# A two-layer graph network: the first layer's one-hot tiles move from VectorE to GpSimd, between its gathers

## The reference

```
h = relu(layernorm(x))
ef = (relu(edge_attr @ We1 + be1) @ We2 + be2) * sigmoid(edge_weight * Wt + bt)
msg = relu(concat(h[src], ef) @ Wn1 + bn1) @ Wn2 + bn2
x = x + h + segment_sum(msg, dst)                  # first layer
g = relu(layernorm(x))
y = g + segment_sum(g[src], dst)
x = x + relu(relu(y @ W1 + b1) @ W2 + b2)          # second layer
```

## Time and profile before

| | |
|---|---|
| median of 3 runs | 2865.11 us |
| the profiled execution: its span, from first to last instruction (no other time of it is recorded) | 3603.9 us |
| mean granted TensorE clock in it | 0.804 of full speed |
| busy share of the span: PE, PEld, DVE, ACT, POOL | 74%, 45%, 54%, 28%, 58% |
| GpSimd: gathers | 2080, 2032.9 us busy, 977 ns mean |
| DMA | 426.82 MB, mean 118 GB/s |

### The profile page before, as it was taken

The page is one execution under the profiler, slowest core; times in us unless marked ns, Lnnn a source line. Parts: engine busy times, 40 slices in busy tenths (PEclk is TensorE's granted clock), DMA queues, the critical chain, the costliest instruction groups (busy, mean ns, idle before and its releaser), DMA issues.

```text
span 3603.9 us, 51709 instructions
## 1 busy us (share of the span) xinstructions
PE 2652.8 (74%) x14584; PEld 1610.3 (45%) x14585; DVE 1962.6 (54%) x4063; ACT 1009.1 (28%) x1000; POOL 2098.5 (58%) x2125
## 2 busy tenths in 40 slices
PE   4687788877877778778877788785645766766766
PEld 3344444444444444444444444343332545544544
DVE  8665566655656566656655566665673333233333
ACT  3233333333333333333333333232231111111112
POOL 6566666666666666666666665555254555555552
PEclk8788888888888888878888888887875777877777
DMA  6444444444433343444344343333122434334332
GB/s 196 113 127 134 127 127 136 125 130 128 126 121 125 123 124 122 123 125 124 120 122 128 120 128 115 120 117 96 32 101 83 132 118 129 122 95 128 101 114 61
DMA packets 229418, 426.82 MB, mean 118 GB/s; under 512 B 82703, under 2 KB 141584, under 8 KB 229072
## 3 DMA queue, kind: packets, MB, share of 16 engines
q0 software_dynamic: 74752, 153.23, 16.3%
q1 hardware_dynamic: 103152, 177.42, 15.0%
q10 hardware_dynamic: 51266, 93.34, 7.4%
HBM read 364.35 MB, written 59.43 MB: 118 GB/s over the span
## 4 chain that ended last, share of the span: by engine, by line
PE 39%; issue 20%; DVE 17%; another core or an unknown queue 12%; DVEq 10%; SPq 1%; DMA 1%; ACT 0%; POOL 0%; ACTq 0%
PE ps L925 9%; PE ps L836 8%; PE ps L795 8%; DVE nodes L1185 5%; PE ps L804 5%; PE ps L815 4%; PE ps L787 3%; DVEq L1119 3%; DVEq L1165 2%; DVE hot L1140 2%; DVE acc L1127 1%; DVE arena L1185 1%; DVEq L1182 1%; PE ps L915 1%
## 5 line engine op out<-in xcount | busy, mean ns | idle before, releaser
L537 POOL DMA_INDIRECT big<-table,idx x2080 | 2032.9, 977 | 1375.8 <-issue 587.6
L836 PE MATMUL ps<-nodes 128*128 128x500 bf16 x1280 | 448.5, 469 | 335.8 <-DVE nodes L1185 180.3
L795 PE MATMUL ps<-arena,we 128*128 128x512 f32 x784 | 511.9, 784 | 29.7 <-issue 12.2
L640 ACT ACTIVATE big<-big 128x1024 f32<-128x1024 f32 x196 | 207.2, 1057 | 1074.3 <-DVE big L1134 917.5
L815 PE MATMUL ps<-hot,big 128*128 128x64 f32 x3136 | 395.9, 275 | 112.8 <-issue 86.0
L1185 DVE TENSOR_SCALAR nodes<-iota_k,win_off,nodes 128x500 bf16<-128x500 f16 x1280 | 453.7, 407 | 0.0
L815 PEld LDWEIGHTS ps<-hot,big 128*128 128x128 f32 x3136 | 381.6, 195 | 107.0 <-issue 104.6
L1182 DVE TENSOR_TENSOR nodes<-iota_b,nodes 128x384 bf16<-128x384 f16 (+1 forms) x492 | 245.4, 499 | 266.8 <-remote 174.8
L1134 DVE TENSOR_TENSOR big<-ps,big 128x1024 f32<-128x1024 f32 x196 | 239.3, 1221 | 244.2 <-issue 242.6
L836 PEld LDWEIGHTS ps<-nodes 128*128 128x128 bf16 x1280 | 106.3, 106 | 573.6 <-DVE nodes L1185 271.1
L630 ACT ACTIVATE arena<-ps,cols 128x1024 f32<-128x1024 f32 x196 | 218.5, 1115 | 418.7 <-PE ps L787 229.2
(11 more groups left out here) (147 smaller groups left out, 2534.2 us busy)
## 6 DMA issues: line engine op xcount, KB each, us to landing
arena<-in_ew SPq DMA_DIRECT2D x196, 512.0 KB
arena<-in_ea SPq DMA_DIRECT2D x196, 256.0 KB
counts_d<-arena ACTq DMA_DIRECT2D x192, 245.0 KB
acc<-counts_d ACTq DMA_DIRECT2D x15, 2940.0 KB
big<-table,idx POOLq DMA_INDIRECT x2080
table<-big SPq DMA_DIRECT2D x7, 672.0 KB, 3.0
idx<-in_src SPq DMA_DIRECT2D x260, 4.0 KB
xs<-in_x SPq DMA_DIRECT2D x7, 448.0 KB, 5.5
```

The lines of the kernel that those rows point to most:

```text
L537: pool.indirect_dma_start(to(u, q, t), None, table, bass.IndirectOffsetOnAxis(ap=idx[:, u, at:at + 1], axis=0))\
L795: pe.matmul(p_ef[q], we2[:, :], hid[:, q, :], start=True, stop=True).then_inc(ef_mm, 1)
L836: m = pe.matmul(to, hots[:, t, :], keys[:, t, :], start=False, stop=True, skip_group_check=True)
```

## The change

GpSimd makes the first layer's one-hots, a tile at a time (`tile_hots`, 128x64, 8 a pair, 1568 in all), and VectorE's `pair_hots0` is gone from this pass (it stays in later sweeps over the edges, which only run for graphs with wide blocks). From the fourth pair on, a one-hot follows each gather: with the gathers of pair p go the one-hots of pair p-3. The last three pairs' one-hots follow the last gather. GpSimd no longer waits for `ef_mm`, and its one wait for `agg_mm` ahead of pair p is for the sums of pair p-5, which used the same half of `hot`. `hot_made` counts tiles instead of blocks, and VectorE tells by `windows_moved` that `rel` is made. TensorE increments `hid_mm`, `ef_mm` and `pre_mm` once a pair by 2, where it did twice by 1. The second layer is as it was.

```diff
+            HOTS_BACK = RING - 1
+            for pair in range(NPAIR):
+                u, b = pair % RING, pair // RING
+                if b:
+                    pool.wait_ge(pre_made, 2 * (pair - RING) + 2)
+                pool.wait_ge(idx_loaded[u], b * 16 + 16)
+                if b:
+                    pool.wait_ge(agg_mm, pair - HOTS_BACK - 1)
+                    pool.sem_inc(pairs_begun, 1)
+                if pair == HOTS_BACK:
+                    pool.wait_ge(windows_moved, 1)
+                for q in (0, 1):
+                    for t in range(TB):
+                        gather_one(table0, to_rows, u, q, t, gathered)
+                        if pair >= HOTS_BACK:
+                            tile_hots(pair - HOTS_BACK, q, t)
+            for pair in range(NPAIR - HOTS_BACK, NPAIR):
+                pool.wait_ge(agg_mm, pair - 1)
+                for q in (0, 1):
+                    for t in range(TB):
+                        tile_hots(pair, q, t)
...
-                    if not free:
-                        pool.wait_ge(ef_mm, b * (2 * RING) + 2 * u)
                     pool.sem_inc(pairs_begun, 1)
-                    gather_block(table0, to_rows, u, 0, gathered)
-                    if not free:
-                        pool.wait_ge(agg_mm, b * RING + (u - 2))
-                    pool.sem_inc(pairs_begun, 1)
-                    gather_block(table0, to_rows, u, 1, gathered)
...
+            def tile_hots(pair, q, t):
+                at = pair * (2 * TB) + q * TB + t
+                pool.tensor_scalar(hot[:, pair % 2, q, t, :], iota_s[:, :], rel[:, at:at + 1], None, ALU.is_equal)\
+                    .then_inc(hot_made, 1)
...
-                    pe.matmul(p_ef[q], we2[:, :], hid[:, q, :], start=True, stop=True).then_inc(ef_mm, 1)
+                    i = pe.matmul(p_ef[q], we2[:, :], hid[:, q, :], start=True, stop=True)
+                i.then_inc(ef_mm, 2)
...
                 if since >= 2:
-                    pair_hots0(b if u >= 2 else b - 1, (u - 2) % RING)
+                    if not first:
+                        pair_hots0(b if u >= 2 else b - 1, (u - 2) % RING)
                     sum_hots(n - 4, u % 2)
```

More of the change, by code:

```diff
@@ L532, in _, with gather_one @@
                 pool.tensor_tensor(x_g, x_g, stages[g % 2], ALU.add).then_inc(xh_made, 1)
+            def gather_one(table, to, u, q, t, landed):
+                at = q * TB + t
+                pool.indirect_dma_start(
+                    to(u, q, t), None, table,
+                    bass.IndirectOffsetOnAxis(ap=idx[:, u, at:at + 1], axis=0))\
+                    .then_inc(landed[u][q], 16)
             def gather_block(table, to, u, q, landed):
                 for t in range(TB):
[L536 to L540, removed]
+                    gather_one(table, to, u, q, t, landed)
             def gather_pair(table, to, u, landed):
@@ L552, in _, with gather_body @@
             pool.wait_ge(table0_stored, 16 * NG)
[L553 to L557, removed]
+            def tile_hots(pair, q, t):
[23 more added lines that the diff above has]
+                        tile_hots(pair, q, t)
+            def gather_body(b):
                 for u in range(RING):
@@ L560, in gather_body @@
                     pool.wait_ge(idx_loaded[u], b * 16 + 16)
-                    if not free:
-                        pool.wait_ge(ef_mm, b * (2 * RING) + 2 * u)
                     pool.sem_inc(pairs_begun, 1)
-                    gather_block(table0, to_rows, u, 0, gathered)
-                    if not free:
-                        pool.wait_ge(agg_mm, b * RING + (u - 2))
-                    pool.sem_inc(pairs_begun, 1)
-                    gather_block(table0, to_rows, u, 1, gathered)
-            for b in range(1, NBODY):
-                gather_body(b, b >= NBODY - 2)
+                    gather_pair(table0, to_rows, u, gathered)
             pool.wait_ge(sweeps_made, 1)
@@ L786, in hidden_products @@
                     k = slice(q * K_EDGE, (q + 1) * K_EDGE)
-                    pe.matmul(p_hid[q], we1[k, :], ea_s[k, u, :], start=True, stop=True).then_inc(hid_mm, 1)
+                    i = pe.matmul(p_hid[q], we1[k, :], ea_s[k, u, :], start=True, stop=True)
+                i.then_inc(hid_mm, 2)
             def edge_products(n, first):
@@ L805, in message_products @@
                                       start=True, stop=True)
-                    i.then_inc(pre_mm, 1)
+                i.then_inc(pre_mm, 2)
             def aggregate(n, m, first):
                 pe.wait_ge(msg_made, n + 2)
-                pe.wait_ge(hot_made, n + 2)
+                pe.wait_ge(hot_made, n * TB + 2 * TB)
                 if not first:
@@ L1113, in _ @@
             first_windows()
+            dve.sem_inc(windows_moved, 1)
             dve.wait_ge(acc_zeroed, 1)
@@ L1140, in pair_hots0 @@
                 dve.tensor_tensor(hot[:, u % 2, :, :, :].rearrange("p q t w -> p (q t) w"), iota_t, r, ALU.is_equal)\
-                   .then_inc(hot_made, 2)
+                   .then_inc(hot_made, 2 * TB)
             def sum_hots(n, m):
-                dve.wait_ge(hot_made, n + 2)
+                dve.wait_ge(hot_made, n * TB + 2 * TB)
                 with nc.allow_low_precision("sums of four zeros and ones"):
@@ L1211, in edge_keys, with pair_step @@
                 settle()
-            def pair_step(s, b, u, since, counted=False):
+            def pair_step(s, b, u, since, first, windows=False):
                 blk = b * (2 * RING) + 2 * u
                 n = s * NB + blk
-                if counted:
+                if windows:
                     window_hots(window_entry(early_group(b, u), VTS[u]), hot_src0, hot_key0, src_b0, key0, VTS[u], VH)
@@ L1257, in sweep @@
                 for u in range(RING):
-                    pair_step(s, 0, u, u)
+                    pair_step(s, 0, u, u, counted)
                     if counted and u < NWG:
@@ L1266, in sweep @@
                         for u in range(RING):
-                            pair_step(s, b, u, RING, True)
+                            pair_step(s, b, u, RING, True, True)
                 else:
@@ L1270, in sweep @@
                         for u in range(RING):
-                            pair_step(s, b, u, RING)
+                            pair_step(s, b, u, RING, False)
                 messages(s * NB + (NB - 4), s, NBODY - 1, RING - 2)
                 add_sums(s * NB + (NB - 6), NB - 6, s * NPAIR + (NPAIR - 2))
-                pair_hots0(NBODY - 1, RING - 2)
+                if not counted:
+                    pair_hots0(NBODY - 1, RING - 2)
                 sum_hots(s * NB + (NB - 4), 0)
@@ L1277, in sweep @@
                 add_sums(s * NB + (NB - 4), NB - 4, s * NPAIR + (NPAIR - 1))
-                pair_hots0(NBODY - 1, RING - 1)
+                if not counted:
+                    pair_hots0(NBODY - 1, RING - 1)
                 sum_hots(s * NB + (NB - 2), 1)
```

## The result

| | us, median | range | runs |
|---|---|---|---|
| kernel before, measured beside the changed one | 2866.45 | 2864.87 to 2877.59 | 4 |
| changed kernel | 3632.01 | 3630.59 to 3636.18 | 4 |
| ratio | 1.268 | 1.265 to 1.270 | |

Slower by 766 us. Predicted were 3200 us, 2860 to 3420. The sign is right, the size is 2.3 times too small, and the time lies outside the range.

The account below looks back on a forecast made before the run. GpSimd's back-to-back gathers were taken to bound both layers of the timed run, some 85% sure. 2865 us plus 329 for the one-hots plus 6 at the layer's end gave 3200, range 2860 to 3420.

Parts of the forecast that it names:

- the sum: Whole kernel before: GpSimd's gathers back to back, plus gaps and ends, 2867.7 us; the second layer's part 644.7.
- Rival C: Whole kernel: GpSimd doesn't bound the timed run, so the kernel gains, 2732 us at best; chance 0.10.
- The one-hot's own cost: First layer, GpSimd: each 128x64 one-hot takes 0.21 us, 329 us for 1568; between 204 and 392 by kind.
- Meetings with VectorE: First layer: one-hots wait for VectorE's use of SBUF, 0.05 us each, 78 us, kept for the range only.
- VectorE's 133.5 us: First layer: one-hots taken off VectorE, 133.5 us less work there, worth nothing while GpSimd bounds.
- the removed waits: First layer: GpSimd's dropped waits for other engines, worth 0 in a timed run, at most 71 us.
- the new waits: First layer: VectorE's sum of pair p-3 waits for pair p's gathers; chain 6.7 to 9.9 us, doesn't decide.
- the increments: TensorE: three fewer increments a pair, worth nothing, since TensorE has 2 us a pair to spare.
- The end of the layer: End of first layer: 24 one-hots after the last gather, 5 us, and a chain of waits; 6 us more.
- B: Between gathers: the one-hot fits in the 0.30 us gap, gathers stay at 1.25; 2871 us, or 2800 to 2875; chance 0.15.
- D: Between gathers: a one-hot prevents the overlap of the next gather's start, 0.81 us each, 4140 us; chance 0.10 with milder form.
- its milder form: First layer: SBUF ports met at each one-hot, 0.41 us each on 2871, 3514 us; shares the 0.10 chance.

Follow-up runs that it names:

- experiment 5: Kernel before with one or four of a pair's eight first-layer gathers left out (0.946, 0.818), or one-column instructions added behind every fourth, second, or every gather (0.994, 0.990, 0.977).
- experiment 2: Changed kernel with the instruction between gathers replaced: 64-column write 3728.46 us, copy 3736.64, one-column comparison 3593.96, comparison with a constant 3764.28.
- experiment 3: Changed kernel with a pair's eight one-hots behind its eight gathers instead of one behind each: 3763.39 us, ratio 1.044 to the kernel before.

## Why the prediction came out as it did

*What bounds.* Borne out for the timed run, which is the first chip's, though no trace shows that run. The changed kernel's second layer is the same code, measured beside it, and took 649.3 us for the 644.7 of the sum, and what the other stages leave for the first layer of before is 1.30 us a gather, near the 1.25 of gathers back to back. Rival C (2732 us) is out. The profile that I read was of the other pace, in which GpSimd's work doesn't bound (experiment 5); the change costs 7% there, and 1.784 us a gather is only 0.17 more than the 1.61 of that profile.

*The one-hot's own cost.* This is the step that failed: "I take 0.21, nearer to the row that reads: 1568 x 0.21 = 329 us", with ends of kind of 0.13 and 0.25. It is 0.45, 706 us, more than twice the 0.21. Neither row was of its kind. IOTA writes only, and experiment 2 shows that a write-only instruction nearly vanishes in a gather's turn. The select's 0.25 us for 128 columns was no ceiling either: a comparison costs 0.285 with a single column, and 2.6 ns more with each further one. The Trainium skill (GPSIMD Engine Reference, section 3.1 "Elementwise — side-by-side cycle accounting") states about 1.8 cycles an element at best and 2.6 with two inputs, at 1.2 GHz; by these figures an element is 1.5 to 2.2 ns, an estimate. The 2.6 ns measured here are 3.1 such cycles, somewhat above.

*Meetings with VectorE.* I kept 78 us for the range and added none. The mean distance of 1.784 is 0.084 above the regular 1.70, 132 us in 1568. The trace of the changed kernel shows where they lie: some 95 us in 435 distances that are less than 1 us too long, and some 38 in nine longer holes, one of 22.9 near the layer's end. Of the 238 distances that are 0.1 to 1 us too long, 237 overlap VectorE's window one-hots (L1204 and, right behind, L1207); of the 1098 regular ones 187 overlap L1204. So the meetings are real, and cost up to 95 us. A timed run of before had 0.033 above 1.25 by the sum, 52 us, so all that was added above the one-hots' 706 is some 80 us. That is the rest that makes up the 785, and no test of it; how many meetings before had already, no trace shows, and by these figures the added ones lie between 40 and 80 us (an estimate). The term of 78 was of the right order, and leaving it out of the sum was an error beside the large one. By the rule of the Trainium skill (SBUF — State Buffer, section "Who interferes with whom") a GpSimd instruction that reads SBUF meets VectorE's instructions with two SBUF inputs; the trace agrees as far as place goes, since the slow one-hot (0.75 for 0.47 us) stands beside L1204, whose two inputs are in SBUF. But more of the delay, 0.59 of 0.70 us, lies between the start of the next gather's record (1.61 for 1.03) and the next one-hot, so the trace doesn't say that only one-hots are held.

*VectorE's 133.5 us, the removed waits, the new waits, the increments.* The first chip's trace bears out that they are worth nothing there: GpSimd waits 33.5 us for VectorE and 0.3 for TensorE. None of them was tried alone on that chip. On the later chips the increments are shown at 1.000, VectorE's one-hots are worth 41 us, and the removed waits are not neutral: taking them out of the kernel before costs 8.7%, with 512 pauses for 281, so they seem to pace GpSimd's gathers there. The new wait does not decide, though VectorE stands behind GpSimd for 1296 us.

*The end of the layer.* Forecast +6, and 88.5 us between the layers for 102.3, so -14: the gap had been read from a trace of the other pace, and what the 24 last one-hots add was not measured by itself.

*The rivals.* B (the one-hot rides in the 0.30) holds for a write and fails for a comparison. The distance of "1.25 us, however long the record" that I held against B misreads the rows: the record of 1.11 us at 1204.06 has 0.30 behind it too, so that distance is 1.41. D came nearest in its milder form, 3514 for 3632, and that was luck, since its mechanism is not what the runs show: experiment 3 leaves 0.04 us for a lost overlap, and the meetings added at most 80 us, where the 0.41 of that form holds 0.20 of meetings on each one-hot, 314 us. The range's upper end, 3420, stood for a one-hot of 0.35 us, and that ceiling had no row of its kind under it.

## What to carry to other kernels

An instruction's price on an engine is that of its kind (reads or only writes, compares or copies) plus its columns; if the trace has no row of the same kind, let the range go far beyond the nearest ones, above all for many short instructions on the engine that bounds. Before work goes to an engine, sum its instructions back to back and compare with the timed run: when the trace and the timed run differ, that sum helps to tell which of the two pictures holds. A wait that looks like waste may pace an engine: take it out alone and measure before counting it as a gain. And where runs on several chips are to be compared, measure the kernel before on each.

## What the runs showed of the hardware

- In a row of gathers, a 128x64 fp32 comparison on GpSimd with a number a partition costs 0.45 us (0.42 in a row of eight of its kind); one column costs 0.285; a 64-column write 0.025; a 64-column copy 0.128 (one run).
- A GpSimd gather of 128 rows repeats every 1.25 us when nothing holds it. With a reading instruction behind it, its record grows from 0.94 to 1.03 and the "issue" ahead of it falls from 0.30 to 0.16: neither is a cost by itself.
- One kernel took 2866 us in the first measurement and 3602 to 3657 us on four chips later. In the longer pace TensorE's records start multiples of 0.70 us apart for some 10 us at a time, in code that waits for nothing, after dense gathers; the cause is open. There, 2.28 us more GpSimd work a pair made the kernel 2.3% faster (ratio 0.972 to 0.981); where there are no pauses it should be slower, by up to 438 us (an estimate), which was not run.
